# Projecting q and k of the third and fourth tile a step earlier, moving token loads and additions forward, and ending a fused attention and expert layer in halves

## The reference

```python
q = sigmoid(heads(Wq, bq)); k = sigmoid(heads(Wk, bk)); v = heads(Wv, bv)
sink_in = normal / einsum(q + EPS, cumsum(k) + EPS)
src_out = normal / einsum(k + EPS, cumsum(q) + EPS)
cons_sink = einsum(q + EPS, cumsum(k * src_out) + EPS) / normal
cons_src = clip(einsum(k + EPS, cumsum(q * sink_in) + EPS) / normal, -1, 1)
sink_alloc = sigmoid(cons_sink); cons_src = exp(cons_src)
src_comp = cons_src / cumsum(cons_src) * normal
kv = cumsum(einsum('bhld,bhlm->bhldm', k, v * src_comp), axis=2)
attn = (einsum('bhld,bhldm->bhlm', q * sink_in / normal, kv) * sink_alloc) @ Wo + bo
h = layernorm(inputs + attn)
layer = layernorm(h + gelu(h @ W1 + b1) @ W2 + b2)
x = _layernorm(x + layer)
# experts: top 2 of 8; out += gate * (relu(x wi + bi + x A_e B_e) wo + bo)
x = _layernorm(x + experts(x))
```

## Time and profile before

| | before |
|---|---|
| runs (us) | 401.02, 401.08, 402.63; median 401.08 |
| the profiled run (us) | 401.43, of which the span is 399.4 |
| PE busy | 368.6 us (92%) |
| DVE busy | 331.3 us (83%) |
| POOL busy | 254.5 us (64%) |
| ACT busy | 211.3 us (53%) |
| granted TensorE clock, mean | 0.995 |
| HBM | 7.29 MB read, 2.10 MB written |

### The profile page before, as it was taken

The page is one execution under the profiler, slowest core; times in us unless marked ns, Lnnn a source line. Parts: engine busy times, 40 slices in busy tenths (PEclk is TensorE's granted clock), DMA queues, the critical chain, the costliest instruction groups (busy, mean ns, idle before and its releaser), DMA issues. The chain is left out here.

```text
span 399.4 us, 6746 instructions
## 1 busy us (share of the span) xinstructions
PE 368.6 (92%) x2086; PEld 261.6 (65%) x2086; DVE 331.3 (83%) x789; ACT 211.3 (53%) x393; POOL 254.5 (64%) x431
## 2 busy tenths in 40 slices
PE   8987999988998999899999999899999997999992
PEld 3565666865657884787668775778477764955651
DVE  2889989988689879998899979997999989834643
ACT  3340047055752896258842885279734873286450
POOL 2023849895489548983798449963898369946131
PEclk9999999999999999999999999999999999999998
DMA  7409043307300028100640038000810064000000
GB/s 255 160 15 221 3 94 91 81 1 173 92 0 2 0 46 211 38 0 2 166 123 2 3 88 202 2 1 20 205 41 1 2 139 98 2 2 27 0 28 26
DMA packets 19875, 26.59 MB, mean 67 GB/s; under 512 B 1664, under 2 KB 9984, under 8 KB 19840
## 3 DMA queue, kind: packets, MB, share of 16 engines
q1 hardware_dynamic: 19696, 25.96, 25.4%
q10 hardware_dynamic: 144, 0.21, 0.2%
HBM read 7.29 MB, written 2.10 MB: 23 GB/s over the span
## 5 line engine op out<-in xcount | busy, mean ns | idle before, releaser
L985 POOL TENSOR_TENSOR prod<-cum_kv,q_fac 128x512 f32<-128x512 f32 x64 | 92.5, 1461 | 19.8 <-DVE cum_kv L1217 14.3
L437 PEld LDWEIGHTS pO<-s_wor,prod 128*128 128x128 f32 x512 | 63.0, 191 | 23.3 <-issue 13.0
L437 PE MATMUL pO<-s_wor,prod 128*128 128x128 f32 x512 | 67.4, 278 | 7.1 <-POOL prod L985 7.0
L1211 DVE TENSOR_TENSOR kv<-k,vb 128x512 f32<-128x512 f32 x64 | 54.3, 849 | 1.4 <-DMA vb<-vs 1.2
L972 POOL TENSOR_TENSOR var_eps<-mv,s_con 128x4 f32<-128x4 f32 x32 | 6.8, 214 | 60.3 <-DVE mv L1239 60.3
L1217 DVE TENSOR_TENSOR_SCAN cum_kv<-p_ones,cum_kv,kv 128x512 f32<-128x512 f32 x32 | 40.6, 1278 | 0.6
L1217 DVE TENSOR_TENSOR_SCAN cum_kv<-p_ones,kv 128x512 f32<-128x512 f32 x32 | 38.8, 1217 | 0.7
L546 PE MATMUL pY<-s_moe,gel 128*128 128x128 f32 x256 | 33.0, 276 | 0.0
L546 PEld LDWEIGHTS pY<-s_moe,gel 128*128 128x128 f32 x256 | 31.0, 192 | 2.9 <-issue 1.9
L456 PE MATMUL pG<-hT,s_ffn 128*128 128x512 f32 x64 | 30.5, 599 | 2.3 <-ACT hT L811 2.2
L975 POOL TENSOR_TENSOR rstd<-var_eps,s_con 128x4 f32<-128x4 f32 x32 | 32.5, 1016 | 0.0
(11 more groups left out here) (180 smaller groups left out, 823.4 us busy)
## 6 DMA issues: line engine op xcount, KB each, us to landing
vb<-vs SPq DMA_DIRECT2D x64, 256.0 KB, 4.6
xT<-x_t SPq DMA_DIRECT2D x8, 256.0 KB, 4.0
xt<-x SPq DMA_DIRECT2D x8, 256.0 KB, 5.1
out<-y SPq DMA_DIRECT2D x7, 256.0 KB, 2.3
s_moe<-moe_w SPq DMA_DIRECT2D x1, 836.0 KB, 10.4
s_wor<-wo_rep SPq DMA_DIRECT2D x1, 512.0 KB, 8.3
...
```

Of the source, the lines that this page charges most:

```text
L437: mm = pe.matmul(pO3[:, s, :], prod[:, m % 4, s * P:(s + 1) * P], s_wor[:, m, :], start=False, stop=(m == DH - 1), skip_group_check=True)
L985: pool.tensor_tensor(prod[:, m % 4, :], cum_kv[t.par][:, m, :], q_fac[t.par][:, :], ALU.mult).then_inc(prod_ready, 1)
L1211: dve.tensor_tensor(kv[:, m % 3, :], k[t.par][:, :], vb[:, m, :], ALU.mult).then_inc(kv_ready, 1)
```

## The change

Four things are changed, and most waits in the diff are there to keep the banks apart.

Projections: q and k of tile 2 move from the start of the third step into the second, into pG1 and pM, in place of two `keep_busy` matmuls; q and k of tile 3 from the start of `step(2)` into the third step, into pG0 and pG1, in place of two more. ScalarE's q_out and k_out move along, and cumulate_q of tile 2 stands ahead of the first moments, both scans of tile 3 ahead of moments(b, 1) in the third step. `den_bank` keeps the denominators of tile 2 in pM and those of tile 3 in pB.

Tokens and additions: `load_xt(Tile(1))` is issued at the start, x_b2n of tile 0 and x_bo of tile 1 are made ahead of the first product.

The constant: `constant_row` stands ahead of its fill, r_cmoe ahead of the first outer product.

The ending: `expert_out` of the last tile is cut in halves. Pieces 0 and 1 go to pY, pieces 2 and 3 to pO, with semaphores of their own, and residuals and statistics follow half by half.

```diff
@@ -192,10 +192,13 @@
 def q_bank(t):
-    return pG[1] if t.n == 1 else pA
+    return pG[0] if t.n == 3 else pG[1] if t.n in (1, 2) else pA
 def k_bank(t):
-    return pM if t.n == 1 else pB
+    return pG[1] if t.n == 3 else pM if t.n in (1, 2) else pB
+def den_bank(t):
+    return pM if t.n in (1, 2) else pB
@@ -212,7 +215,7 @@
 def p_den(t):
-    return k_bank(t)[:, SUMS_AT:SUMS_AT + 2 * HW]
+    return den_bank(t)[:, SUMS_AT:SUMS_AT + 2 * HW]
@@ -322,6 +327,7 @@
     sp.dma_start(s_gb[:, :], gate_row.to_broadcast([P, EXPERTS])).then_inc(gb_loaded, 16)
+    load_xt(Tile(1))
     load_xT(Tile(2))
@@ -329,7 +335,7 @@
         if B: spread_vs(b, 4); spread_vs(b, 5); spread_vs(b, 6)
-        if A and a.n >= 1: load_xt(a)
+        if A and a.n >= 2: load_xt(a)
         if B: spread_vs(b, 7)
@@ -344,24 +350,34 @@
     def project_q(t):
         pe.wait_ge(xT_loaded[t.par], 16 * (t.slot_uses + 1))
-        if t.n > 1:
+        if t.n == 2:
+            pe.wait_ge(q_ready, t.n)
+        elif t.n == 3:
+            pe.wait_ge(gelu_ready, 3)
+        elif t.n > 3:
             pe.wait_ge(qfac_ready, t.n)
-        if t.n == 3:
-            pe.wait_ge(hsum_ready, 1)
         pe.matmul(q_bank(t)[:, :], att("wq"), xT[t.par][:, :], start=True, stop=True).then_inc(q_proj, 1)
...
         pe.wait_ge(xT_loaded[t.par], 16 * (t.slot_uses + 1))
-        if t.n > 1:
+        if t.n == 2:
+            pe.wait_ge(rden_ready, t.n)
+            pe.wait_ge(cmoe_ready, 1)
+        elif t.n == 3:
+            pe.wait_ge(gelu_ready, 4)
+        elif t.n > 3:
             pe.wait_ge(vs_ready, t.n)
-        if t.n == 3:
-            pe.wait_ge(hsum_ready, 2)
         pe.matmul(k_bank(t)[:, :], att("wk"), xT[t.par][:, :], start=True, stop=True).then_inc(k_proj, 1)
...
             pe.wait_ge(v_ready, t.n)
-        elif t.n > 1:
+        elif t.n == 2:
+            pe.wait_ge(qfac_ready, t.n)
+        elif t.n == 3:
+            pe.wait_ge(qfac_ready, t.n)
+            pe.wait_ge(hsum_ready, 1)
+        elif t.n > 3:
             pe.wait_ge(q_ready, t.n + 1)
@@ -375,7 +391,10 @@
         src, at = (kq, HW) if of_q else (qk, 0)
-        dst = k_bank(t) if pair == 0 else pB
+        if t.n == 3 and pair == 0 and of_q:
+            pe.wait_ge(vs_ready, t.n)
+            pe.wait_ge(hsum_ready, 2)
+        dst = den_bank(t) if pair == 0 else pB
         for s in reversed(range(SUB)):
@@ -442,6 +461,8 @@
             pe.wait_ge(v_ready, 2)
+        elif t.n == 1:
+            pe.wait_ge(q_ready, 4)
         wait(pe, hsum_ready, FC * (t.n - 2) + 3)
@@ -451,6 +472,10 @@
             wait(pe, hsum_ready, FC * (t.n - 1))
+            if t.n == 0:
+                pe.wait_ge(q_ready, 3)
+            elif t.n == 1:
+                pe.wait_ge(k_ready, 4)
         if f >= 2:
@@ -546,6 +571,17 @@
         mm.then_inc(wo_done, 1)
+    def expert_half(t, f, h):
+        pe.wait_ge(hsum_ready, FC * t.n + f + 1)
+        if f == 0 and h == 0:
+            pe.wait_ge(res_ready[3], t.n)
+        elif f == 0:
+            pe.wait_ge(u1T_ready, t.n + 1)
+        for s in (2 * h, 2 * h + 1):
+            mm = pe.matmul((pY3, pO3)[h][:, s, :], hsum[:, f, s * P:(s + 1) * P], wo[:, f, :],
+                           start=(f == 0 and s == 2 * h), stop=(f == FC - 1), skip_group_check=True)
+        mm.then_inc(wo_half_done[h], 1)
@@ -584,8 +620,8 @@
         denominators_T(b, 0); denominators_T(b, 1)
+        constant_row()
         keep_busy(3)
-        constant_row()
         pe.wait_ge(y_free[0], 16)
@@ -595,9 +631,10 @@
         reduce_out(b, 1)
-        keep_busy(2)
+        project_q(a.plus(1))
+        keep_busy(1)
         head_sums(a, 1, False)
-        keep_busy(1)
+        project_k(a.plus(1))
         reduce_out(b, 2)
@@ -615,10 +652,8 @@
     def third_step(c):
         b, a = c.plus(1), c.plus(2)
-        project_q(a); project_k(a)
-        keep_busy(1)
         project_v(a)
-        keep_busy(2)
+        keep_busy(3)
         pe.wait_ge(y_free[1], 16)
@@ -637,9 +672,9 @@
         head_sums(a, 1, False)
-        keep_busy(1, pM)
+        project_q(a.plus(1))
         reduce_out(b, 5)
-        keep_busy(1, pM)
+        project_k(a.plus(1))
         cumulate_e(a)
@@ -680,9 +716,10 @@
         inter2(c, 0); inter2(c, 1)
-        expert_out(c, 0); inter2(c, 2)
-        expert_out(c, 1); inter2(c, 3)
-        expert_out(c, 2); expert_out(c, 3)
+        expert_half(c, 0, 0); expert_half(c, 0, 1); inter2(c, 2)
+        expert_half(c, 1, 0); inter2(c, 3)
+        expert_half(c, 2, 0); expert_half(c, 1, 1)
+        expert_half(c, 3, 0); expert_half(c, 2, 1); expert_half(c, 3, 1)
@@ -705,7 +742,7 @@
         A, B, C, D = a.exists(), b.exists(), c.exists(), d.exists()
-        if A: project_q(a); project_k(a)
+        if A and a.n > 3: project_q(a); project_k(a)
         if D: inter_base(d, 2); inter1(d, 2); inter_base(d, 3); inter1(d, 3)
@@ -881,13 +918,14 @@
     def second_step(b):
         a = b.plus(1)
+        q_out(a.plus(1))
         source_exp(a); alloc_tanh(a); allocation(a)
         spread_scale(a, False); spread_scale(a, True)
+        k_out(a.plus(1))
...
         b, a = c.plus(1), c.plus(2)
-        q_out(a); k_out(a)
         normalise(c, 0); v_out(a); seed_x(b); h_out(c)
@@ -936,7 +976,7 @@
         A, B, C, D = a.exists(), b.exists(), c.exists(), d.exists()
-        if A: q_out(a); k_out(a)
+        if A and a.n > 3: q_out(a); k_out(a)
         if D: relu(d, 2); relu(d, 3)
@@ -1049,19 +1089,24 @@
+    def opening(a):
+        e_normal(a); attention_input(a); shifted_x(a)
+        attention_input(a.plus(1))
+        product(a, 0)
     def second_step(b):
         a = b.plus(1)
-        product(b, 1); attention_input(a); product(b, 2)
-        product(b, 3); product(b, 4)
+        product(b, 1); product(b, 2); product(b, 3)
         e_normal(a)
-        product(b, 5); product(b, 6); product(b, 7)
+        product(b, 4); product(b, 5); product(b, 6); product(b, 7)
...
         inverse_std(c, 0); scaled_h(c); h_residual(c)
-        product(b, 0); product(b, 1); shifted_x(c); product(b, 2); product(b, 3)
+        product(b, 0); product(b, 1); product(b, 2); product(b, 3)
         attention_input(a)
@@ -1086,7 +1131,7 @@
         if B: scaled_n2(b)
-    step(Tile(-1))
+    opening(Tile(0))
     second_step(Tile(0))
@@ -1326,6 +1371,20 @@
+    def half_residual(t, h):
+        dve.wait_ge(wo_half_done[h], FC)
+        dve.wait_ge(x2c_ready, t.n + 1)
+        dve.wait_ge(norm_ready[3], SUB * t.n)
+        for s in (2 * h, 2 * h + 1):
+            ins = dve.scalar_tensor_tensor(res[3][:, s, :], (pY3, pO3)[h][:, s, :], gate_sum[t.par][:, s:s + 1],
+                                           x2c[:, s, :], ALU.mult, ALU.add)
+        ins.then_inc(res_half_ready[h], 1)
+    def half_moments(h):
+        dve.wait_ge(res_half_ready[h], 1)
+        for s in (2 * h, 2 * h + 1):
+            dve.bn_stats(stats[3][:, s, :], res[3][:, s, :]).then_inc(stats_ready[3], 1)
     dve.wait_ge(att_loaded, 16)
@@ -1349,7 +1408,9 @@
             second_relu(c, f)
-        expert_residual(c); moments(c, 3)
+        half_residual(c, 0); half_moments(0)
+        half_residual(c, 1); half_moments(1)
+        join_moments(c, 3)
         dve.wait_ge(shift_ready[3], c.n + 1)
@@ -1392,6 +1453,9 @@
         sink(b); cumulate_sink(b); k_times_cum_q(b, 1)
+        dve.wait_ge(row_loaded, 16)
+        dve.wait_ge(cmoe_mm, 1)
+        dve.scalar_tensor_tensor(r_cmoe[:, :], row("bffn"), 2.0, pM[:, 0:P], ALU.mult, ALU.add).then_inc(cmoe_ready, 1)
         outer_product(a, 0); cumulate_kv(a, 0); outer_product(a, 1)
@@ -1411,16 +1475,14 @@
         values(a); query_factor(a)
+        cumulate_q(a.plus(1))
         dve.wait_ge(gb_loaded, 16)
-        dve.wait_ge(row_loaded, 16)
-        dve.wait_ge(cmoe_mm, 1)
-        dve.scalar_tensor_tensor(r_cmoe[:, :], row("bffn"), 2.0, pM[:, 0:P], ALU.mult, ALU.add).then_inc(cmoe_ready, 1)
...
         moments(c, 0)
-        cumulate_q(a); cumulate_k(a); k_times_cum_q(a, 0); q_times_cum_k(a, 0)
+        cumulate_k(a); k_times_cum_q(a, 0); q_times_cum_k(a, 0)
         outer_product(b, 0); cumulate_kv(b, 0)
@@ -1448,6 +1510,7 @@
         outer_product(a, 2); cumulate_kv(a, 2); outer_product(a, 3)
+        cumulate_q(a.plus(1)); cumulate_k(a.plus(1))
         moments(b, 1)
@@ -1462,7 +1525,7 @@
         if B: cumulate_kv(b, 7)
-        if A: cumulate_q(a); cumulate_k(a)
+        if A and a.n > 3: cumulate_q(a); cumulate_k(a)
         if D: second_relu(d, 2); second_relu(d, 3)
...
         if C: gate(c, 0)
```

2 lines of the change are left out of this document (added).

## The result

| | before | after |
|---|---|---|
| runs beside each other, median (us) | 401.78 (401.02 to 402.63, 8 runs) | 403.51 (402.95 to 404.94, 8 runs) |
| ratio to before | 1 | 1.0047, 95% interval 1.0034 to 1.0059 |
| span of the profiled run (us) | 399.4 | 400.8 |
| granted TensorE clock, mean | 0.995 | 0.988 |

The forecast was 400.4 with a range up to 401.9. The time went the other way, out of the range. The forecast was counted from the first three runs of before, 401.08; against the 401.78 of all eight its -0.65 would be 401.1, and the miss is the same: +1.73 came where -0.65 stood.

What follows compares the result with a forecast made beforehand. VectorE bounds 30 to 56 us, TensorE 62.3 to 83.5, then layer norms, then TensorE in the loop. 0.3 - 0.1 + 0.05 + 0.3 + 0 - 1.2 = -0.65 us, from 401.08 to 400.4; range 398.0 to 401.9.

Steps and rivals of the forecast that it cites:

- Rival 2: TensorE's clock falls in the longer 3.5 us wait before tile 1's x2_T, costing 2.7 us: 403.1 us; chance 0.06.
- Fourth step: 0: Work shed ahead of tile 1's x2_T only lengthens TensorE's wait, 1.77 to 3.5 us; two scans fit idle time; 0.
- Third step: Up to 83.5 us, +0.05 us: two matmuls shed ahead of h_T worth nothing, `shift` +0.25, x_bo of tile 2 -0.2.
- Opening, +0.3: Before the first kv: r_cmoe moved there costs about 0.2 us, x_b2n pieces beside rden_n 0.1; +0.3 us together.
- Second step, -0.1: Up to tile 1's rcum_e: product 2's earlier start gains 0.75 us, blocked VectorE work takes it back; -0.1 us.
- The choice on `clipped`: Second step: product 3 on GpSimd blocks `clipped` until 43.6, so the term is -0.1 us; unblocked, -0.9.
- rival 1: VectorE and GpSimd meet well: kv goes first, saving 1.0 us, and `clipped` is unblocked, 0.8: 398.6 us; chance 0.29.
- cumulate_q and the third step, +0.05: Tile 2's scan fills idle time, 0 us, VectorE's 1.2 us lead lost by q_sink; then +0.05 up to 83.5 us.
- The collision with `shift`: Third step: earlier kq and qk fall on GpSimd's `shift` and lengthen it, +0.25 us, from 0 to 0.5.
- The 0.3 for k_out: k_out, some 0.6 us long, stands ahead of tile 0's x2 on ScalarE and delays x2_T: +0.3 us.
- Halves, -1.2: Ending: first half's residuals and statistics run during the last 8 matmuls, 1.0 us, plus 0.2: -1.2 us, 0.8 to 1.4 saved.
- The 0.2 for the last relu's wait: Ending: last inter2 comes ahead of half an expert piece, so the wait for the last relu shrinks, saving 0.2 us.

Runs made afterwards that it cites:

- fill_both: The changed kernel with two fill matmuls ahead of tile 1's x2_T and five instead of three in the opening; 400.15 us, ratio 0.9970.
- proj3_fill: The kernel before with only tile 3's projections moved into the third step, and two fill matmuls ahead of tile 1's x2_T; 402.20 us, ratio 1.0014.

## Why the prediction was wrong, point by point

**The clock: the step that failed.** Rival 2 named the mechanism and had a chance of 0.06, and the step "Fourth step: 0 ... The wait only grows, to 3.5" priced the growth at nothing. The wait did grow, to 3.47, as the forecast said, and the growth was the damage. Two things were wrong in the weighing. It took 2.65 us as a wait that the full clock outlives, from one execution: that was chance, as by the mean clocks it falls behind just that wait in 58 of 91 runs of before. A threshold cannot be read from one trace. And it looked for a fall in one place only; there were two in the profile after. The price of a fall was set too high (2.7, by 5.4 us of work at half speed): measured, the slow stretch lasts some 3.4 us and costs 1.48 and 1.66. So 403.1 came close to 403.51 by two errors that cancel in part. Leaving the rival out of the range was the error of the range. The same step, work moved away and the wait left open, was taken once more in "Third step": "TensorE sheds two matmuls ahead of h_T ... worth nothing" opened the 1.37 us behind which the clock fell in the third place.

**Opening, +0.3.** Right in kind: from the factors' first matmul to the first reduce_out it is 7.38 after and 7.19 before (28.62 to 35.81), +0.19. That this made the first wait 2.85 and not 2.65 was not seen; all eight runs of after are at .981 to .989, as two falls give, so the fall there now came every time or nearly so.

**Second step, -0.1.** The choice on `clipped` was right: where the clock stays up it meets product 3 and takes 0.94 (42.27 in fill_both, 42.60 in proj3_fill), as the Trainium skill's page SBUF — State Buffer, section Who interferes with whom, has it. In the profile after it took 0.19, since the fall had made `cons` late and the product was over. Wrong was the other half: the kv behind it came 0.02 after the product in fill_both (44.44 and 44.42) and 0.03 in after (45.60 and 45.57) and was not held, though the prediction had it blocked; it took 0.66, and the product took 1.81. That is the gain of 1.0 that rival 1 wanted. From the first reduce_out to rcum_e it is 11.45 in fill_both and 12.62 before: -1.17 where -0.1 stood. In the changed kernel the fall took it back: rcum_e at 48.88, 0.45 later than before.

**cumulate_q and the third step, +0.05.** The lead was lost at q_sink as said (0.77 of waiting at 72.33). The collision with `shift` did not come: 0.20 at 59.24, not 0.45 to 0.58. From tile 0's first moments to x2_T of tile 1 it is 65.72 in fill_both and 65.58 before, +0.14 where +0.35 was forecast, k_out's 0.34 being in it. The 0.3 for k_out was right.

**Fourth step, scans.** They fitted into the idle time: 3.24 before, 0.88 now at 109.13.

**Halves, -1.2.** Measured 0.77, just under the lower end of 0.8. The first half's residuals could start only 0.86 ahead of the last matmul's end (393.01, 393.87), and cut in halves the work up to mv takes 2.20 where in one piece it took 2.07 (391.72 to 393.79), starting 0.04 behind the last matmul's end: 0.86 + 0.04 - 0.13 = 0.77, where 1.0 stood. The 0.2 for the last relu's wait did not show: from the last x2_T to the last matmul's end it is 20.41 in both kernels.

**The sum by measured terms**, on the span: start of the opening -0.23 (28.39, 28.62, which differs from run to run), front without falls -0.77, falls +1.66 and +1.48, behind +0.04, ending -0.77: +1.41, against 400.8 - 399.4 = 1.4. Without the falls and the start it is -1.50 where the forecast had -0.65: the front did better than its +0.55 by 1.3 us and the ending worse than its -1.2 by 0.4. Had the clock stayed up, the forecast would have come near the time by these two errors, which go in opposite directions.
